# A perceiver kernel on one core: the local-attention slot in another order on three engines, six evictions moved, and widening in five and a half units

## The reference, cut to what matters

```python
for i in range(6):
    x = attn_layer(shift_tokens(x), Wqkv[i], q_scale[i], k_scale[i], Wo[i]) + x
    x = ffn_layer(shift_tokens(x), ln_g[i], ln_b[i], W1[i], b1[i], W2[i], b2[i]) + x

def attn_layer(x, Wqkv, qs, ksc, Wo):          # 16 heads of 64
    q, k, v = split(x @ Wqkv)                  # 256 -> 3 * 1024
    q, k = l2norm(q) * qs, l2norm(k) * ksc     # then rotary, scaled
    return local_attention(q, k, v) @ Wo       # windows of 64, one window back

def ffn_layer(x, g, bln, W1, b1, W2, b2):
    xn = (x - mu) / sqrt(var + 1e-05) * g + bln
    a, gate = split(xn @ W1 + b1)              # 256 -> 2 * 682
    return a * gelu(gate) @ W2 + b2            # 682 -> 256
```

## Time and profile before

| | us |
|---|---|
| median of 3 runs | 2459.87 |
| the profiled execution | 2458.22 |
| span of its trace | 2456.4 |
| first slot starts on TensorE | 917.3 |
| mean granted clock of TensorE | 0.964 of full |

### The profile page before, as it was taken

The page is one execution under the profiler, slowest core; times in us unless marked ns, Lnnn a source line. Parts: engine busy times, 40 slices in busy tenths (PEclk is TensorE's granted clock), DMA queues, the critical chain, the costliest instruction groups (busy, mean ns, idle before and its releaser), DMA issues.

```text
span 2456.4 us, 50282 instructions
## 1 busy us (share of the span) xinstructions
PE 2218.1 (90%) x16450; PEld 1722.7 (70%) x16450; DVE 1753.9 (71%) x4875; ACT 1318.3 (54%) x3952; POOL 454.7 (19%) x272
## 2 busy tenths in 40 slices
PE   4899999999996758999999999999999999999986
PEld 3677777777764536777777777777777777777765
DVE  5886786786773657787778777787778677877752
ACT  1655364464550036566567666766667666756541
POOL 2101011010010022122223222322223212211210
PEclk9999999999998969999999999999999999999988
DMA  3000000000003000011011001101110111011000
GB/s 105 7 9 1 10 5 5 6 5 5 23 0 116 22 9 12 12 63 29 27 31 63 12 28 46 63 12 30 46 63 12 31 46 61 14 29 42 8 12 20
DMA packets 45287, 70.18 MB, mean 29 GB/s; under 512 B 7314, under 2 KB 32004, under 8 KB 44804
## 3 DMA queue, kind: packets, MB, share of 16 engines
q1 hardware_dynamic: 42692, 62.33, 8.3%
q10 hardware_dynamic: 2368, 4.98, 0.6%
HBM read 50.54 MB, written 1.05 MB: 21 GB/s over the span
## 4 chain that ended last, share of the span: by engine, by line
PE 43%; ACT 11%; DVE 4%; issue 4%; DMA 1%; DVEq 0%; ACTq 0%; SPq 0%; POOL 0%; POOLq 0%
PE ps_loc L1605 10%; PE ps_loc L1504 7%; ACT prob_loc L1754 7%; PE ps_loc L1577 6%; PE ps_loc L1616 5%; PE ps_loc L1566 4%; PE ps_loc L1552 3%; PE ps_loc L1523 3%; PE ps_loc L1541 2%; ACT qk L1733 2%; DVE prob_loc L1972 2%; ACT pT L1761 1%; DVE stats_loc L2006 1%; DMA late<-y_all 1%; ACT v_loc L1733 1%
## 5 line engine op out<-in xcount | busy, mean ns | idle before, releaser
L1504 PE MATMUL ps_loc<-w_high,xT 128*128 128x512 f32 x1152 | 399.5, 429 | 5.8 <-DVE w_low L1899 4.3
L2190 POOL TENSOR_TENSOR rnorm<-norm_floor,half_loc 128x32 f32<-128x32 f32 x48 | 262.5, 5469 | 537.3 <-DVE norm_floor L1910 454.3
L1754 ACT ACTIVATE prob_loc<-prob_loc,top_loc 128x128 f32<-128x128 f32 x768 | 297.7, 391 | 25.1 <-DVE top_loc L1972 22.8
L1972 DVE CUSTOM_DVE_ANT_0 prob_loc<-ps_loc,const,rnorm 128x128 f32<-128x128 f32 x768 | 223.0, 347 | 118.0 <-PE ps_loc L1541 92.9
L1605 PE MATMUL ps_loc<-xnT_loc,w 128*114 128x256 f32 (+1 forms) x1152 | 264.8, 384 | 1.2 <-ACT xnT_loc L1776 1.2
L631 ACT ACTIVATE prob<-prob,new_top 128x256 f32<-128x256 f32 x512 | 252.1, 495 | 0.0
L1504 PEld LDWEIGHTS ps_loc<-w_high,xT 128*128 128x128 f32 x1152 | 201.1, 194 | 70.8 <-issue 29.1
L1504 PE MATMUL ps_loc<-w_low,xT 128*128 128x512 f32 x576 | 231.5, 402 | 0.0
L1605 PEld LDWEIGHTS ps_loc<-xnT_loc,w 128*114 128x114 f32 (+1 forms) x1152 | 201.5, 179 | 42.5 <-ACT xnT_loc L1776 1.8
L1746 ACT ACTIVATE qT_loc<-ps_loc 128x512 f32<-128x512 f32 x96 | 57.4, 598 | 284.0 <-PE ps_loc L1523 284.0
L822 DVE COPY probT<-ps_cross 128x512 f32<-128x512 f32 x256 | 164.5, 684 | 38.6 <-PE ps_cross L449 36.7
(11 more groups left out here) (180 smaller groups left out, 4614.5 us busy)
## 6 DMA issues: line engine op xcount, KB each, us to landing
w_raw<-in_ffn_Wqkv_dram SPq DMA_DIRECT2D x24, 512.0 KB, 5.4
v_mid<-v_loc SPq DMA_DIRECT2D x48, 256.0 KB, 3.4
w<-in_ffn_W_dram SPq DMA_DIRECT2D x24, 341.0 KB, 4.5
w_raw<-in_ffn_Wqkv_dram SPq DMA_DIRECT2D x24, 256.0 KB, 4.0
wo<-in_ffn_Wo_dram SPq DMA_DIRECT2D x24, 256.0 KB, 3.8
ctx_raw<-in_ctx_dram SPq DMA_DIRECT2D x12, 256.0 KB, 2.7
late<-y_all SPq DMA_DIRECT2D x24, 127.0 KB
w<-in_ffn_W_dram SPq DMA_DIRECT2D x12, 228.0 KB
```

Of the source, the lines that this page charges most:

```text
L1504: ins = pe.matmul(ps[:, DENSE + j % 2, :], xT[:, px, kk, t * P:(t + 1) * P], wqkv[pw][:, kk, col:col + 512], start=kk == 0 and n == 0, sto ...
L1754: ins = act.activation(pr, pr, ACT.Exp, bias=top[:, h, t:t + 1], scale=-1.0, accum_out=total[:, h, t:t + 1])
L1972: ins = dve.tensor_tensor_reduce(out=prob[:, 2 * (pair % RING) + e, t, :], in0=ps[:, score_bank(pair, e), t * P:(t + 1) * P], in1=band, sc ...
L2190: pool.tensor_tensor(rnorm[:, b % 2, t, :], norm2_floor[:, :], half[:, :], ALU.pow).then_inc(rnorm_done, 8)
```

## The change

Four things, all in `local_layers` or in what it loads:

1. `slot` has a new order on TensorE, ScalarE and VectorE. The first transposition of probabilities comes after `scores(3)` and not after `project(5)`; pairs and projections alternate otherwise; `turn_probs(7)` stands behind `widen(1)`; `widen(2)` and `widen(3)` stand among the last pairs. On VectorE `moments` and `normal` stand later, `add_attention` ahead of the last three rotary pieces, and `weights_low` of pieces 2 and 3 moves from the `split` slot to the `late` slot.
2. `o_out` of pairs 0 to 5 moves from ScalarE to VectorE; pairs 6 and 7 stay.
3. FWIDE is 128 five times and 42, and the last unit's value and gate halves are computed in one group of matmuls: W1 lies in memory as 682 value columns, 22 zero columns and the last 42 gate columns, then the other 640 gate columns. So `widen(5)` has two matmuls of 106 columns and not four of 113; `narrow` takes all 128 rows, and W2's last block is zeroed first.
4. The reciprocal is taken in place in `total`; `rtotal` is gone.

```diff
-FWIDE = [FF // FM + (m < FF % FM) for m in range(FM)]
+FWIDE = [min(P, FF - m * P) for m in range(FM)]
+REST = FWIDE[-1]
+GATE_REST = FF - REST + DH
+GATE_MAIN = GATE_REST + REST
...
-                for part in range(2):
+                for part in range(2 if m < FM - 1 else 1):
+                    col = part * GATE_MAIN + FAT[m]
+                    n = P if m < FM - 1 else DH + REST
                     for kk in range(KD):
-                        ins = pe.matmul(ps[0:n, DENSE + m % 2, part * T:(part + 1) * T],
-                                        w1[:, kk, part * FF + FAT[m]:part * FF + FAT[m] + n], xnT[:, kk, :],
+                        ins = pe.matmul(ps[0:n, DENSE + m % 2, part * T:(part + 1) * T], w1[:, kk, col:col + n], xnT[:, kk, :],
                                         start=kk == 0, stop=kk == KD - 1)
...
+            def o_out(a, pair):
+                if pair == 0:
+                    dve.wait_ge(y_full, a)
+                dve.wait_ge(o_full, a + 2 * (pair + 1))
+                dve.tensor_copy(oT[:, pair, :], ps[:, OUT, 0:T]).then_inc(o_done, 2)
...
+                inverse(a, 3)
+                share(a, 2)
+                if late:
+                    weights_low(L + LAYER, 5)
+                if ahead:
+                    norms(n, 0)
+                    twists(n, nL, 0, 0)
+                share(a, 3)
+                minima(a, b, 6)
+                inverse(a, 4)
+                o_out(a, 1)
...
+                    gated(f, 5)
+                if split:
+                    weights_low(L + LAYER, 0)
+                add_attention(a, b)
                 if ahead:
                     cosines(n, 1, 0)
-                if ffn:
-                    gated(f, 5)
-                if ahead:
-                    scaled_keys(n, (b + 1) % B, 0)
                     q_sum(n, 1)
                     scaled_keys(n, (b + 1) % B, 1)
```

More of the change, by code:

```diff
@@ L186, in load_layer_weights @@
             for kk in range(KD):
-                for j in range(2):
-                    cut = slice(j * FF, (j + 1) * FF)
-                    eng.dma_start(self.w1[:, kk, cut], src[one, :, kk, cut].rearrange("o p n -> (o p) n")).then_inc(self.w1_in, 16)
+                eng.dma_start(self.w1[:, kk, 0:FF], src[one, :, kk, 0:FF].rearrange("o p n -> (o p) n")).then_inc(self.w1_in, 16)
+            for at, cut in ((GATE_MAIN, slice(FF, 2 * FF - REST)), (GATE_REST, slice(2 * FF - REST, 2 * FF))):
+                eng.dma_start(self.w1[:, :, at:at + cut.stop - cut.start], src[one, :, :, cut].rearrange("o p k n -> (o p) k n"))\
+                    .then_inc(self.w1_in, 16)
         else:
@@ L1764, in o_out @@
             def o_out(a, pair):
-                if pair == 0:
-                    act.wait_ge(y_full, a)
                 act.wait_ge(o_full, a + 2 * (pair + 1))
@@ L1844, in slot @@
                     gates(f, 0)
-                o_out(a, 6)
-                probs_out(a, 7)
+                probs_out(a, 6)
                 if ffn:
                     gates(f, 1)
+                probs_out(a, 7)
+                o_out(a, 6)
+                if ffn:
+                    gates(f, 2)
+                    gates(f, 3)
                 o_out(a, 7)
                 if ffn:
-                    for m in range(2, FM):
-                        gates(f, m)
+                    gates(f, 4)
+                    gates(f, 5)
                 if split:
@@ L1980, in inverse @@
                 dve.wait_ge(exp_done, a + 2 * (pair + 1))
-                dve.reciprocal(rtotal[:, two, :], total[:, two, :]).then_inc(rtotal_done, 2)
+                dve.reciprocal(total[:, two, :], total[:, two, :]).then_inc(rtotal_done, 2)
             def share(a, pair):
@@ L2055, in slot @@
                 if late:
-                    weights_low(L + LAYER, 4)
+                    weights_low(L + LAYER, 2)
                 minima(a, b, 0)
+                if late:
+                    weights_low(L + LAYER, 3)
                 if b == 1:
                     layer_vectors(L, i)
+                minima(a, b, 1)
+                minima(a, b, 2)
+                inverse(a, 0)
+                share(a, 0)
                 if ffn:
                     moments(f, fb, shifts)
-                minima(a, b, 1)
+                inverse(a, 1)
@@ L2063, in slot @@
+                minima(a, b, 3)
+                share(a, 1)
+                if late:
+                    weights_low(L + LAYER, 4)
+                minima(a, b, 4)
                 if ffn:
                     normal(f, fb)
-                minima(a, b, 2)
-                inverse(a, 0)
-                for pair in range(3, PAIRS):
-                    minima(a, b, pair)
-                    inverse(a, pair - 2)
-                    share(a, pair - 3)
-                    if late and pair == 3:
-                        weights_low(L + LAYER, 5)
-                    if ahead and pair == 5:
-                        norms(n, 0)
-                    if ahead and pair == 6:
-                        twists(n, nL, 0, 0)
@@ L2077, in slot @@
-                inverse(a, PAIRS - 2)
-                share(a, PAIRS - 3)
+                inverse(a, 2)
+                minima(a, b, 5)
+                o_out(a, 0)
+                inverse(a, 3)
+                share(a, 2)
+                if late:
+                    weights_low(L + LAYER, 5)
+                if ahead:
+                    norms(n, 0)
[4 more added lines that the diff above has]
+                o_out(a, 1)
@@ L2079, in slot @@
                 if ahead:
                     twists(n, nL, 0, 1)
-                inverse(a, PAIRS - 1)
-                share(a, PAIRS - 2)
-                share(a, PAIRS - 1)
+                o_out(a, 2)
+                inverse(a, 5)
+                share(a, 4)
+                share(a, 5)
+                minima(a, b, 7)
+                o_out(a, 3)
                 if ahead:
                     cosines_both(n, 0)
-                    sums(n, 0)
+                o_out(a, 4)
+                inverse(a, 6)
@@ L2087, in slot @@
+                share(a, 6)
+                if ahead:
                     norms(n, 1)
@@ L2089, in slot @@
                     x_low(L + U * (b + 2))
+                o_out(a, 5)
+                inverse(a, 7)
+                share(a, 7)
                 if ffn:
                     gated(f, 0)
-                if ahead:
-                    twists(n, nL, 1, 0)
-                if ffn:
                     gated(f, 1)
                 if ahead:
-                    twists(n, nL, 1, 1)
+                    sums(n, 0)
                 if ffn:
@@ L2116, in slot @@
                 if split:
-                    weights_low(L + LAYER, 0)
-                add_attention(a, b)
-                if split:
-                    for c in range(1, 4):
-                        weights_low(L + LAYER, c)
+                    weights_low(L + LAYER, 1)
                 if ffn:
@@ L2164, in _ @@
             pool.memset(half[:, :], -0.5)
-            for buf in (zero[:, :], late[0:1, :, :]):
+            for buf in (zero[:, :], late[0:1, :, :], w1[:, :, FF:GATE_REST]):
                 ins = pool.memset(buf, 0.0)
```

90 lines of the change are left out of this document (45 added, 45 removed).

## The result

The changed kernel takes 2386.14 us (median of 6 runs, 2382.51 to 2391.84); the kernel before, on the same chip, 2460.36 (2459.02 to 2464.55). The ratio is 0.9696, 95% interval 0.9682 to 0.9711. The forecast was 2379, in a range of 2361 to 2411: the likeliest case came true, 7 us above its figure.

A forecast was written before the change was run, and what follows sets the result against it. The chain was taken to run almost wholly on TensorE, bounded by its pieces' lengths and its standstills. Terms summed to -79.5 us from 2458.2, giving 2379 us, in a range of 2361 to 2411.

The forecast's parts named there:

- (a): Widening on TensorE: four trace rows of 0.219 us go in each of 24 feed-forward parts, -21.0 us.
- (b): TensorE's waits for transposed probabilities ahead of the first and fourth values products vanish in the steady slots, -53.9 us.
- (c): Low-clock stretches behind the long waits go with them: 11 times 1.53 us, -16.8 us.
- (d): New TensorE wait at `turn_probs(7)`, its eviction queued behind Gelu and table load: 0.70 us in 23 slots, +16.1 us.
- (e): Six evictions moved to VectorE stay hidden, the tightest place having 0.35 us to spare: 0 us.
- (f): Five `late` slots: VectorE brings eviction 1 at 26.7 us, TensorE is there at 25.7; 1.0 us each, +5.0 us.
- (h): First slot, bound by VectorE: evictions and the sum into y join its queue, +1.8 us, bounds 0 and 2.7.
- (C): Rival: new short waits keep the clock falling in half of the slots, so 2396 us; chance 0.15.
- (D): Rival: no wait at `turn_probs(7)`, because the table load starts earlier than read, so 2363 us; chance 0.12.
- (j): Taken at nothing: among others, three rotary pieces behind `add_attention` are covered by W2, about 0.7 us to spare.
- (B): Rival: waits move to handoffs between VectorE and TensorE, 1.3 us a slot more, +30, 2409 us; chance 0.20.
- (F): Rival: the half unit saves nothing, held by `gates(4)` and the shared bank, +21, 2400 us; chance 0.04.

The follow-up runs named there:

- half unit alone: The kernel before with only the narrow last widening unit, its memory layout and the in-place reciprocal, orders and evictions unchanged: 2432.49 us, ratio 0.9876.
- evictions on ScalarE: The changed kernel with the six `o_out` of pairs 0 to 5 moved from VectorE back to ScalarE: 2383.33 us, ratio 0.9678 to the kernel before.
- The swap: The changed kernel with the two semaphore waits of every Gelu in the other order: 2372.99 us, ratio 0.9635 to the kernel before.
- share first: The changed kernel with share(3) ahead of `norms` and the first twist behind eviction 1 on VectorE: 2381.01 us, ratio 0.9669 to the kernel before.

## Why the prediction was right, and where its sizes were off

The terms as they came out, in us:

| term | forecast | measured | from |
|---|---|---|---|
| (a) half unit | -21.0 | -20 | half unit alone, 0.85 in 24 parts |
| (b) two waits | -53.9 | -53.9 | no L1573 wait for pT left |
| (c) clock | -16.8 | about -9 | 37 us at the low level, now 17 |
| (d) wait at turn_probs(7) | +16.1 | +14 | 0.95 from start to start in 15 slots, 0.76 of it idle |
| (e) six evictions | 0 | 0 | evictions on ScalarE |
| (f) late slots | +5.0 | about +13 | 312.9 for five, less 5 x 59.08 (58.13 and the 0.95 of (d)), less 3 for two low stretches and 1 that the late slots had over 61.96 before |
| (g) minima | -5.7 | -5.7 | the 1.9 left lie in the last slot |
| (h) first slot | +1.8 | +3.7 | 49.93, now 53.67 |
| (i) last slot | -5.0 | -6.1 | first widening 27.7 in, was 33.8 |
| not foreseen: order | 0 | about -10 | 0.45 in 22 slots |

They sum to about -74; the profiles have -75.2.

**(a) and (b)** were right in mechanism and size. Both could be read to 0.1 us from single rows of TensorE, which does nothing else in those places.

**(c)** held in direction. Half of the low time went. Of the four stretches left, two stand behind the pair of waits in late slots, one behind a wait of 1.92 us in `turn_qk` (1.65 in that slot before), and the longest at the start of the second slot, behind the new wait of 4.45 us (one as long stood in that slot before). So rival (C) is a part of the truth. The term was also counted high: the eleventh of its stretches lies in the last slot, which is no steady slot. And the reason that I gave, that the low level comes with the long wait, is too simple: with all long waits kept, the half unit alone lost nearly half of it.

**(d)** had the length right (0.76 idle where it said 0.70) and the number wrong: 15 slots, not 23. It took from one slot of before that the table load waits for widening 0 and applied it to all, though 8 of the 23 in the trace of before did not wait, as here in the slot that starts at 1222.4:

```profile
1261.33 1.28 ACT L1784 ACT_TABLE_LOAD   x1
```

In the looped slots of b = 0 and 1 the load isn't bound to that unit, and rival (D) came true there. The swap shows that the order of two waits decides this, and that the whole term could be avoided.

**(f)** is the term that failed in size, 1.0 us a slot where about 2.7 came. TensorE's side of it was right: without the two waits it would have stood at the third values product 25.7 us into the slot, as forecast. The step that failed is the sum of VectorE's queue up to eviction 1: 26.7 us forecast, 27.6 measured (the row behind the eviction starts at 1361.21, the slot at 1333.64). A margin of 1.0 us was taken as the difference of two sums near 26, and the one sum was 0.9 short, in small parts: the first minima start 0.2 later, `moments` takes 1.87 with 0.5 of waiting for its own results, and the inverses and shares take 0.4 more together. With 0.1 for the handoff, the eviction is 2.1 us late, and that is the two waits together, 1.19 + 0.92 = 2.11. That share(3) stands ahead of it in the same queue did not add to this: VectorE has no idle time over 0.15 us from 1346.98 to 1361.21, so nothing that TensorE does there holds it up, and the wait for share(3) is a part of the 2.1 us taken earlier. From start to start the pair of waits costs 2.4 us, and `turn_qk`, whose evictions stand behind `weights_low` of piece 1, takes 0.3 more. The runs with less work in the queue bear this out: with one piece of 1.14 us gone there is one wait of 0.92 us, with two pieces gone there is none. Another order (share first) and fewer evictions left the slots at about 62.

**(e)** was right, and the reason for it as well: ScalarE or VectorE, the evictions hide on either.

**(h)** took +1.8 for queueing of evictions. They cost 0.1 there (with the evictions on ScalarE the slot is 53.5 us); 2.7 of the 3.7 are the three rotary pieces behind the sum, which (j) took as covered by W2, and the other 1.0 stays open. In the first slot there is no W2. The cover was named and the one slot without it was not looked for.

**(B), (E)**: new waits of TensorE for VectorE came only in the late slots and around the first and the last; in normal slots all margins held, the 0.35 us one among them. (Three waits of 1.7 to 1.9 us in `turn_qk` of looped slots of b = 0 were there before.) **(F)** is refuted by the half unit alone.

The low end of the range is not the sum that the prediction names: the low bounds of (d), (f), (h) and (i) alone give 2362 us, and with (D) in place of the bound of (d) 2353. The measured time doesn't hang on it.

**Open:** a steady slot without waits went from 59.43 (61.96 less 2.53) to 58.13 us, 0.45 more than the half unit gives. Of this 0.12 is how waits are counted: from start to start the two cost 2.65 us and not 2.53 (from the last row of the projection to the product it is 2.34 and 0.97 us, and 0.33 where there is no wait). For the other 0.33 the new order is what remains as the cause, but no run isolates it; fewer changes from one kind of matmul to another is a guess. Open too is what, beside a wait's length, brings the low level.

## What to carry to other kernels

When an in-order queue runs without a pause, its last late handoff sets the whole loss, and earlier waits only take a part of it sooner; exchanging pieces moves the waits, and only less work shortens them. A margin of 1 us between two sums of 26 us is no better than the sums, so add up every row of one, small ones and pauses too. Ask of each cover in which stage it is missing, and of each wait in which stage it stands: the first slot had no W2, and in a third of the slots the table load was early. And where an activation that changes the function table waits for two semaphores, look in the trace, in every kind of slot, at which wait the table load takes; that one exchange of lines was worth some 14 us here.

## What the runs showed of the hardware

- Which of two waits is written first decided whether the table load (1.28 us) ran beside TensorE's work or behind it: 0.76 us of idle time in 15 slots. The wait written last stood ahead of the table load in these.
- GpSimd subtracts 128x1024 in 2.37 us, VectorE in 1.22. VectorE's took 3.13 us beside it and ended 1.1 us after GpSimd. A VectorE piece that began 0.3 us after GpSimd's had ended took 1.22.
- A copy of 128x256 from PSUM took 0.42 us on VectorE and 0.38 on ScalarE.
- Waits of TensorE of 0.41 to 0.86 us had no low clock behind them (21 slots with three waits each); waits of 1.95 us had it in 10 of 21 slots in one kernel, in 4 of 21 in another, whose slots were 0.85 us shorter. A pair of about 1.2 and 0.92 us had it in 2 of 5.
- Idle time read from the trace understates a wait of TensorE: 0.76 us behind two units of widening cost 0.95 from start to start, 0.58 us behind a projection 0.64.
